# Evening out VectorE's work over the slots of an attention body, and moving ScalarE's loads, in a two-layer decoder kernel

## The chip, the cores and the metric

The kernel runs on one core of a Trainium2 chip. The metric is the device time of one execution in microseconds (us). Three executions of the kernel before took 2007.12, 2007.74 and 2007.95 us; the median is 2007.74.

## The reference: what is computed

```python
# B=16 sequences, S=256 tokens, H=512, 16 heads of 32; fp32 throughout
ln = layernorm(x, ln1);   q, k, v = split(ln @ w_qkv + b_qkv)
x  = x + merge(softmax(mask(q @ k.T / sqrt(32))) @ v) @ w_ao + b_ao          # layer 1: self attention
ln = layernorm(x, ln2);   q = ln @ w_q + b_q;   k, v = split(ctx @ w_kv + b_kv)
x  = x + merge(softmax(mask(q @ k.T / sqrt(32))) @ v) @ w_co + b_co          # layer 2: cross attention
x  = x + gelu(layernorm(x, ln3) @ w1 + b1) @ w2 + b2                         # perceptron
# non-local block over x and ctx: theta, phi, g projections, W = theta.T phi / 512, y = W g, scale, + x
```

All matrix products of fp32 values are made from two halves each (`_h` and `_l`, upper and lower part), as three matmuls: high*high, high*low, low*high (`product`, lines 64 to 68).

## The kernel before, in words

The batch of 16 sequences is cut into 8 blocks of two sequences (512 tokens: four row tiles of 128). The program has three stages:

- 16 short steps at the start (`step`) that fold weights of the non-local block.
- **Attention**: 17 bodies, k = 0 to 16. Bodies 0 to 7 do self attention of blocks 0 to 7, bodies 8 to 15 cross attention, body 16 drains. Each body has eight **slots**, h = 0 to 7.
- The perceptron and the rest of the non-local block (`m_slot`).

A slot treats one group of four heads in a pipeline that is several groups deep. TensorE turns the exponentials of the group before (L1071, out `A_tp`), runs two units of the projections (`units_at`: q and k in slots 0 to 3, two v tiles in slots 4 and 6, two output tiles o in slots 5 and 7), then the scores of a coming group (L1055) and last the weighing of the values (L1089). VectorE multiplies the scores by the mask (L1656), takes maxima (L1666), inverts row sums, scales the weighed values (`scaled`, L1694, out `A_cx`), writes one head's exponentials in 32x32 blocks (L1686), and takes the lower halves of q and k out of PSUM (L1639, `A_q_l`, `A_k_l`) or adds the output tile to the residual (L1634, `A_res`). ScalarE makes the exponentials (L1309, eight per slot, n = 0 to 7), copies turned tiles out of PSUM (L1368) and takes the upper halves.

The units of a slot and the weighing use two PSUM banks in turn: the first unit of a slot needs the bank of the second unit of the slot before (so v0 in slot 4 waits until `A_k_l` of k3 is done, and q0 in slot 0 until `A_res` of o3 is done), the second unit needs the bank whose `A_cx` VectorE makes in the same slot.

Beside that each body prepares the next one's normalised rows. VectorE takes row statistics (`row_statistics`, L1604), GpSimd normalises (L774), VectorE turns the rows in 32x32 blocks (L1814, `A_x<-A_x`), ScalarE's queue writes them to HBM in an order that completes the transposition (`write_block`, L1361, `turned<-A_x`, four DMAs of 64 KB per row tile), and SyncE's queue loads them back (`load_pair`, L734, `A_e<-turned` or `A_xt_l<-turned`).

DMAs are issued by SyncE (SPq in the profile, DMA queue q1) and by ScalarE (ACTq, queue q10), in program order on each. In each slot SyncE issues `A_pt<-exponentials` (256 KB, what the weighing of this slot reads), the store of the inverses, the store of the exponentials, and `A_rt<-inverses` (four DMAs; the next slot's `A_cx` needs them). In slots 5 and 6 it also issues `load_pair`, a row tile and the stores of the output. ScalarE's queue has the loads of `load_row` (`A_x<-x`), `load_res` (`A_res<-x`), masks and contexts; each stands in the program behind one of the exponentials, at a place (h, n). Body 7 also takes in the weights of layer 2 in 16 chunks (`chunk_at`, `load_at`): ScalarE makes the upper half, VectorE the lower half of chunks of w_q, GpSimd of the others. Source line numbers are those of the profile of the kernel before.

Of the kernel before, what the change touches and what calls it, by code (L numbers as in the profile page):

```python
# [18 lines left out]
TT = TOK // P  # L19
NB = B // BPB  # L20
# [7 lines left out]
DMA = 16  # L28
# [109 lines left out]
def whole_network(nc, ctx, nl, m1t_dram, inv_dram, p_dram, xt_dram, rows, x1, x2, ctx_t, s_mask, x_mask, s_weights, x_weights, fold_wt, columns,  # L138
# [12 lines left out]
    NU = 2 * NB  # L151
# [5 lines left out]
    EARLY = 6  # L157
    WARM = 14
    KEPT = range(GROUPS - 12, GROUPS)

    with ExitStack() as stack:
        room = Room(nc, stack, "A")
# [144 lines left out]
        def hidden_bank(blk, f):  # L307
# [7 lines left out]
        load_at = {(7, 0): (0, 1), (7, 3): (2, 3), (7, 5): (4, 5), (7, 6): (6, 7), (7, 7): (8,), (8, 0): (9,), (8, 1): (10, 11),  # L315
                   (8, 2): (12,), (8, 3): (13, 14, 15)}

        made, half_ok, ld_c = room.sem("made"), room.sem("half_ok"), room.sem("ld_c")
# [442 lines left out]
        def _(pool):  # L761
# [94 lines left out]
            def slot(r, k, h, a_, b_, own, pv):  # L856
# [405 lines left out]
        def _(act):  # L1262
# [70 lines left out]
            def load_o_copy(t):  # L1333
                act.dma_start(turned_w[KT + t], fold_wt[3][t * P:(t + 1) * P, :]).then_inc(ld_tw[t], DMA)

            def loads(k, r, h, n):

                if by_blocks(k - 1) and (h, n) in ((0, 3), (0, 4), (1, 3)):
                    load_row(k + 1, r + 1, 2 * h + n - 2)
                if NB <= k + 1 < NU and n == 4 and h in (1, 2):  # L1340
                    load_context(r + 1, h - 1)
                if NB <= k < NU and (h, n) == (3, 5):
                    load_mask(r, 1)
                if NB <= k < NU - 1 and (h, n) == (7, 3):
# [12 lines left out]

# [206 lines left out]
        def _(dve):  # L1564
# [176 lines left out]
            def step(n):  # L1741
# [29 lines left out]
                if n in (7, 11, 15):  # L1771
                    biases_of((n - 7) // 4)

            def slot(r, k, h, a_, b_, own, pv):
                even, odd = turns_at(k, h)
                coming, leaves = exists(k, h, 1), exists(k, h, -2)
# [31 lines left out]
                    lower_pair(k, r, halves_at(k, h))  # L1808
                if k == NU and h in (0, 2):
                    lower_pair(k - 1, r - 1, h // 2)  # L1810
                if by_blocks(k) and h in (3, 4) or k == NU - 1 and 3 <= h < 3 + TT:
                    for t in (2 * h - 6, 2 * h - 5) if by_blocks(k) else (h - 3,):
                        dve.wait_ge(ln_x, (r + 1) * TT + (t + 1))
                        dve.transpose(x[:, t, :], x[:, t, :]).then_inc(a_blk, 1)  # L1814
                if k < NU and h in ((0, 1) if k else (1, 2)):
                    row_statistics(r + 1, 0 if h == (0 if k else 1) else 2)
                    row_statistics(r + 1, 1 if h == (0 if k else 1) else 3)
                if k == 0 and h == 2:
                    aggregate(r + 1)
# [13 lines left out]
                    split_raw(3, O_SPLITS[h])  # L1833
                for n in chunk_at.get((k, h), ()):
                    split_chunk(n)
                if k == NU and h == EARLY:
                    early_chunks = m_chunk_at[(k, h)]
                    for f in range(2, EARLY):
                        if f >= 4:
                            split_m_chunk(early_chunks[f - 4])  # L1840
                        activated(0, f, True)
                    for n in early_chunks[2:]:
                        split_m_chunk(n)
                    dve.wait_ge(m1_hi, 1)
                    dve.tensor_tensor(thw_l[:, :], m1[:, :], f32(thw_h[:, :]), ALU.subtract).then_inc(m1_lo, 1)
# [160 lines left out]
```

## Time and profile before

| | us |
|---|---|
| median of 3 executions | 2007.74 |
| the profiled execution | 2011.13 |
| its span, first to last instruction | 2009.3 |
| TensorE busy in it | 1976.2 (98%) |
| VectorE busy | 1470.8 (73%) |
| ScalarE busy | 1162.6 (58%) |
| GpSimd busy | 550.2 (27%) |

The span leaves out 1.83 us of the execution. Durations below are those of this one execution. Matmuls overlap in the pipeline, so a matmul row's length is not what it costs: the distance between starts is. Attention takes from about 107 to 1259 us of the span. In the profile, groups name tiles as out<-in; buffer numbers are left out. PEld is the weight load that goes before a matmul.

### The profile page before, as it was taken

The numbers are of one execution on the slowest core, as the hardware profiler recorded it, in microseconds if no ns is written. First come the engines' busy times: TensorE is split into PE (matmuls) and PEld (weight loads), VectorE is DVE, ScalarE is ACT, GpSimd is POOL, SyncE is SP. The second block draws the span as 40 slices with busy tenths as digits, with TensorE's granted clock in tenths as the row PEclk, the third lists the DMA queues.
The fourth block names the chain that finished last, engine by engine and source line by source line (L and its number), as shares of the span: only waits on it lengthen the run. The fifth ranks groups of instructions, "written<-read, shape, count | busy, mean of one in ns | idle before, by whom it ended". The sixth has DMA issues, their size and how long they took to land. (4 is left out here: it accounts for less than half of the span.)

```text
span 2009.3 us, 41550 instructions
## 1 busy us (share of the span) xinstructions
PE 1976.2 (98%) x13632; PEld 1570.0 (78%) x13632; DVE 1470.8 (73%) x3868; ACT 1162.6 (58%) x3251; POOL 550.2 (27%) x556
## 2 busy tenths in 40 slices
PE   9999999999999999999999998999999999999998
PEld 8877777777776777777777776888888888888887
DVE  7799999999999999899899888564444343435333
ACT  4388878888888888888888788421111121212111
POOL 1012222222224344323423432053132131313000
PEclk9999999999999999999999999999999999999999
DMA  8546667567668867767767734531212212121201
GB/s 279 168 94 139 146 165 155 128 168 161 135 173 193 195 172 173 168 162 180 176 152 183 170 90 116 171 107 35 79 42 68 68 47 78 47 63 52 61 24 48
DMA packets 681720, 252.67 MB, mean 126 GB/s; under 512 B 533312, under 2 KB 626112, under 8 KB 681536
## 3 DMA queue, kind: packets, MB, share of 16 engines
q1 hardware_dynamic: 535616, 195.84, 38.5%
q10 hardware_dynamic: 145920, 54.55, 11.2%
q8 instruction: 95, 1.56, 0.3%
q14 instruction: 89, 0.73, 0.1%
HBM read 167.41 MB, written 82.84 MB: 125 GB/s over the span
## 5 line engine op out<-in xcount | busy, mean ns | idle before, releaser
L1309 ACT ACTIVATE A_p<-A_p,A_nmax 128x256 f32<-128x256 f32 x1024 | 507.1, 500 | 5.4 <-DVE A_res L1634 1.7
L1666 DVE CUSTOM_DVE_ANT_0 A_p<-A_p,A_ma 128x256 f32<-128x256 f32 x1024 | 376.6, 423 | 4.6
L1656 DVE TENSOR_TENSOR A_p<-A_sc,A_mk 128x1024 f32<-128x1024 f32 x256 | 312.3, 1220 | 48.0 <-PE A_tp L1071 47.4
L820 POOL TENSOR_TENSOR A_ct_l<-A_cx,A_ct_h 128x256 fp32r<-128x256 f32 x122 | 114.3, 937 | 652.3 <-DVE A_nmax L1666 639.1
L1368 ACT ACTIVATE A_pt<-A_tp 128x512 f32<-128x512 f32 x396 | 218.5, 588 | 47.2 <-PE A_tp L1071 45.9
L1071 PEld LDWEIGHTS A_tp<-A_ident,A_p 128*128 128x128 f32 x1584 | 178.8, 141 | 71.2 <-ACT A_p L1309 33.0
L1071 PE MATMUL A_tp<-A_ident,A_p 128*128 128x128 f32 x1584 | 222.5, 277 | 1.5 <-DVE A_xt_l L1617 0.7
L1505 ACT ACTIVATE A_mk<-A_tp,A_cols 128x512 f32<-128x512 f32 x62 | 42.8, 690 | 269.1 <-PE A_tp L68 269.0
L1309 ACT ACTIVATION_READ_ACCUMULATOR A_p<-A_p,A_nmax 128x1 f32 x1024 | 197.2, 193 | 0.0
L1505 ACT ACTIVATE A_ma<-A_tp,A_cols 128x512 f32<-128x512 f32 x62 | 42.8, 690 | 242.5 <-PE A_tp L68 242.5
L66 PE MATMUL A_banks<-A_xt_h,A_w_h 128*128 128x512 f32 x384 | 162.2, 422 | 3.4 <-DVE A_res L1634 2.1
L929 POOL TENSOR_TENSOR A_v<-A_v,A_b_row 128x512 f32<-128x512 f32 x32 | 52.7, 1664 | 362.3 <-DMA A_v<-x 362.3
L68 PE MATMUL A_banks<-A_xt_h,A_w_l 128*128 128x512 f32 x384 | 151.1, 394 | 0.0
L67 PE MATMUL A_banks<-A_xt_l,A_w_h 128*128 128x512 f32 x384 | 150.1, 391 | 0.0
L1857 DVE CAST A_h_h<-A_ma 128x512 fp32r<-128x512 f32 x64 | 30.5, 476 | 160.4 <-ACT A_ma L1505 156.7
L1375 ACT ACTIVATE A_cx<-A_cx,A_bias_sum 128x256 f32<-128x256 f32 x128 | 65.2, 510 | 139.8 <-DVE A_cx L1694 139.7
L66 PE MATMUL A_tp<-A_xt_h,A_w_h 128*128 128x512 f32 x368 | 143.4, 390 | 0.2 <-DVE A_xt_l L1871 0.2
L67 PE MATMUL A_tp<-A_xt_l,A_w_h 128*128 128x512 f32 x368 | 143.2, 389 | 0.0
L68 PE MATMUL A_tp<-A_xt_h,A_w_l 128*128 128x512 f32 x368 | 143.2, 389 | 0.0
L1089 PE MATMUL A_banks<-A_pt,A_v 128*32 128x256 f32 x2048 | 137.9, 387 | 4.8 <-DMA A_pt<-exponentials 2.1
L1857 DVE CAST A_h_h<-A_mk 128x512 fp32r<-128x512 f32 x64 | 29.1, 454 | 143.6 <-ACT A_mk L1505 141.5
L66 PE MATMUL A_banks<-A_w_h,A_ct_h 128*128 128x512 f32 x256 | 105.7, 413 | 1.6 <-issue 1.1
(248 smaller groups left out, 5001.7 us busy)
## 6 DMA issues: line engine op xcount, KB each, us to landing
exponentials<-A_ln_shift SPq DMA_DIRECT2D x464, 64.0 KB, 2.7
A_pt<-exponentials SPq DMA_DIRECT2D x116, 256.0 KB, 3.1
A_rt<-inverses SPq DMA_DIRECT2D x512, 32.0 KB, 2.4
x<-A_res SPq DMA_DIRECT2D x64, 256.0 KB, 3.6
A_res<-x ACTq DMA_DIRECT2D x58, 256.0 KB, 4.1
turned<-A_x ACTq DMA_DIRECT2D x224, 64.0 KB, 2.8
A_x<-x SPq DMA_DIRECT2D x54, 256.0 KB, 3.7
A_x<-x ACTq DMA_DIRECT2D x42, 256.0 KB, 3.1
```

What stands on the lines that cost most here:

```text
L66: pe.matmul(out, sh, mh, start=first, stop=False)
L67: pe.matmul(out, sh, ml, start=False, stop=False)
L68: return pe.matmul(out, sl, mh, start=False, stop=last)
L820: pool.tensor_tensor(ct_l[:, f, part], cx[:, :], f32(ct_h[:, f, part]), ALU.subtract).then_inc(c_lo, 1)
L1071: last = pe.transpose(tp[:, n % 2, c * S + t * P:c * S + (t + 1) * P], p[:, g % 2, j, t, c * P:(c + 1) * P], ident[:, :])
L1089: last = pe.matmul(banks[rr, bank, 0:S], v[:, b * TPB + c, f * P + j * HD:f * P + (j + 1) * HD], turned_keys(grp, j, c), start=(c == 0), s ...
L1309: act.activation(p[:, g % 2, j, t, :], p[:, g % 2, j, t, :], ACT.Exp, scale=-1.0, bias=nmax[:, g % 2, j, t:t + 1], accum_out=rsum[:, g % 2 ...
L1368: act.activation(pt[:, moved(grp) + i, :, :], tp[:, n % 2, :].rearrange("p (c s) -> p c s", c=TPB), ACT.Copy)\
L1375: act.activation(cx[:, :], cx[:, :], ACT.Identity, bias=bias_sum[:, layer(k, h, -2), 2, f:f + 1]).then_inc(c_sum, 1)
L1505: act.activation(hf[f % 4], hidden_bank(blk, f), ACT.Gelu_apprx_tanh, bias=b1_col[:, f:f + 1])\
L1656: dve.tensor_tensor(p[:, g % 2, heads, :, :].rearrange("p j t s -> p j (t s)"), sc[:, heads, :], m, ALU.mult)\
L1666: dve.tensor_tensor_reduce(out=a_, in0=a_, in1=ma[:, b, t, :], scale=-1.0, scalar=BIG, op0=ALU.add, op1=ALU.min, accum_out=nmax[:, g % 2, ...
```

## The change

Four things are moved, all in the attention bodies:

1. **VectorE.** In bodies 1 to 14 the four block transposes of the rows stood as two in slot 3 and two in slot 4; now one stands in slot 3, two in slot 4, one at the end of slot 5. The statistics of row tile 0 move from slot 0 to the end of slot 6 of the body before.
2. **ScalarE's stores of turned rows** follow: tile 0 in slot 4, tiles 1 and 2 in slot 5, tile 3 in slot 6 (before: 0 and 1 in slot 4, 2 and 3 in slot 5).
3. **ScalarE's loads** (rows, contexts, masks, residuals, the copies of w_o) go behind the last exponential (n = 7) of a slot, and some to another slot: row tiles 1, 2, 3 from slots 0, 0, 1 to slots 6 and 7 of the body before and slot 0; residual tiles 0 and 1 from slot 2 to slots 0 and 3, tiles 2 and 3 from slot 6 to slot 6 and the start of slot 7.
4. **Body 7.** The first two bias additions of GpSimd go from slot 4 to slot 1 (their loads to slot 0), and the loads of weight chunks 4 and 5 from SyncE's queue (slot 5) to ScalarE's, behind the last exponential of slot 5.

```diff
+    EARLY_ADDS = (NB - 1, NU - 1)
...
-        load_at = {(7, 0): (0, 1), (7, 3): (2, 3), (7, 5): (4, 5), (7, 6): (6, 7), ...
+        load_at = {(7, 0): (0, 1), (7, 3): (2, 3), (7, 6): (6, 7), ...
...
-                if h == (4 if 1 < k < NU - 1 else 1) and k:
+                if h == (1 if k in (1, *EARLY_ADDS) else 4) and k:
                     add_bias(k - 1, r - 1, 0)
                     add_bias(k - 1, r - 1, 1)
...
-                if by_blocks(k) and h in (4, 5):
-                    write_block(k, r, 2 * h - 8 + n // 4, n % 4)
+                tile = {(4, 0): 0, (5, 0): 1, (5, 1): 2, (6, 0): 3}.get((h, n // 4))
+                if by_blocks(k) and tile is not None:
+                    write_block(k, r, tile, n % 4)
...
-                if by_blocks(k - 1) and (h, n) in ((0, 3), (0, 4), (1, 3)):
-                    load_row(k + 1, r + 1, 2 * h + n - 2)
-                if NB <= k + 1 < NU and n == 4 and h in (1, 2):
+                if by_blocks(k) and (h, n) in ((6, 7), (7, 7)):
+                    load_row(k + 2, r + 2, h - 5)
+                if by_blocks(k - 1) and (h, n) == (0, 7):
+                    load_row(k + 1, r + 1, 3)
+                if NB <= k + 1 < NU and n == 7 and h in (1, 2):
                     load_context(r + 1, h - 1)
-                if NB <= k < NU and (h, n) == (3, 5):
+                if NB <= k < NU and (h, n) == (3, 7):
                     load_mask(r, 1)
-                if NB <= k < NU - 1 and (h, n) == (7, 3):
+                if NB <= k < NU - 1 and (h, n) == (7, 7):
                     load_mask(r + 1, 0)
-                if 1 < k < NU and h == (2 if k < NU - 1 else 0) and n in (5, 6):
-                    load_res(k - 1, r - 1, n - 5)
-                if 0 < k < NU and h == 6 and n in (5, 6):
-                    load_res(k - 1, r - 1, n - 3)
+                if 1 < k < NU and (h, n) in (((0, 7), (3, 7)) if k not in EARLY_ADDS else ((0, 5), (0, 6))):
+                    load_res(k - 1, r - 1, int((h, n) in ((3, 7), (0, 6))))
+                if 0 < k < NU and (h, n) in ((6, 7), (7, 0)):
+                    load_res(k - 1, r - 1, h - 4)
+                if k == NB - 1 and (h, n) == (5, 7):
+                    for c in (4, 5):
+                        load_chunk(c)
-                if k == 2 and (h, n) in ((1, 5), (2, 3), (3, 3), (6, 4)):
+                if k == 2 and (h, n) in ((1, 5), (2, 7), (4, 7), (5, 7)):
...
-                if by_blocks(k) and h in (3, 4) or k == NU - 1 and 3 <= h < 3 + TT:
-                    for t in (2 * h - 6, 2 * h - 5) if by_blocks(k) else (h - 3,):
-                        dve.wait_ge(ln_x, (r + 1) * TT + (t + 1))
-                        dve.transpose(x[:, t, :], x[:, t, :]).then_inc(a_blk, 1)
+                if k == NU - 1 and 3 <= h < 3 + TT:
+                    row_blocks(r, h - 3)
+                if by_blocks(k):
+                    for t in {3: (0,), 4: (1, 2)}.get(h, ()):
+                        row_blocks(r, t)
                 if k < NU and h in ((0, 1) if k else (1, 2)):
-                    row_statistics(r + 1, 0 if h == (0 if k else 1) else 2)
+                    if h != 0 or k < 2:
+                        row_statistics(r + 1, 0 if h == (0 if k else 1) else 2)
                     row_statistics(r + 1, 1 if h == (0 if k else 1) else 3)
...
+                if by_blocks(k) and h == 5:
+                    row_blocks(r, 3)
+                if by_blocks(k) and h == 6:
+                    row_statistics(r + 2, 0)
```

`row_blocks(r, t)` is the wait and the transpose that stood in the loop; `load_chunk` on ScalarE waits for the same semaphores and issues the same DMA as SyncE's.

VectorE at the end of slot 3 of a self-attention body, before (`A_k_l` is the lower half of k3, which frees the bank that v0 needs):

```order
1476 L1666 ISA A_p,A_nmax<-A_p,A_ma 128x256
1477 L1666 ISA A_nmax 128x1
1478 L1814 STREAM_TRANSPOSE A_x<-A_x 128x512 x2
1479 L1639 SCALAR_TENSOR_TENSOR A_k_l<-A_banks,A_bias_sum,A_k_h 128x512
1480 L1656 TENSOR_TENSOR A_p<-A_sc,A_mk 128x1024
```

The same place after the change:

```order
1488 L1681 ISA A_p,A_nmax<-A_p,A_ma 128x256
1489 L1681 ISA A_nmax 128x1
1490 L1792 STREAM_TRANSPOSE A_x<-A_x 128x512
1491 L1654 SCALAR_TENSOR_TENSOR A_k_l<-A_banks,A_bias_sum,A_k_h 128x512
1492 L1671 TENSOR_TENSOR A_p<-A_sc,A_mk 128x1024
```

One transpose stands before `A_k_l` instead of two.

ScalarE from the start of slot 6 of a cross-attention body (body 10) to the start of slot 7, before:

```order
1223 L1309 ACTIVATE A_p,A_rsum<-A_p,A_nmax 128x256 x2
1224 L1368 ACTIVATE A_pt<-A_tp 128x512 x2
1225 L1375 ACTIVATE A_cx<-A_cx,A_bias_sum 128x256
1226 L1378 ACTIVATE A_ct_h<-A_cx 128x256
1227 L1309 ACTIVATE A_p,A_rsum<-A_p,A_nmax 128x256
1228 L1368 ACTIVATE A_pt<-A_tp 128x512
1229 L1301 ACTIVATE A_v<-A_banks 128x512
1230 L1309 ACTIVATE A_p,A_rsum<-A_p,A_nmax 128x256 x2
1231 L1283 ACTIVATE A_xt_h<-A_xt_l 128x4x256
```

The same stretch after the change:

```order
1150 L1310 ACTIVATE A_p,A_rsum<-A_p,A_nmax 128x256
1151 L1376 DMA turned<-A_x 32x16x32
1152 L1310 ACTIVATE A_p,A_rsum<-A_p,A_nmax 128x256
1153 L1376 DMA turned<-A_x 32x16x32
1154 L1383 ACTIVATE A_pt<-A_tp 128x512 x2
1155 L1390 ACTIVATE A_cx<-A_cx,A_bias_sum 128x256
1156 L1393 ACTIVATE A_ct_h<-A_cx 128x256
1157 L1310 ACTIVATE A_p,A_rsum<-A_p,A_nmax 128x256
1158 L1376 DMA turned<-A_x 32x16x32
1159 L1383 ACTIVATE A_pt<-A_tp 128x512
1160 L1302 ACTIVATE A_v<-A_banks 128x512
1161 L1310 ACTIVATE A_p,A_rsum<-A_p,A_nmax 128x256
```

Four stores of row tile 3 now stand in slot 6, one behind each of its first four exponentials (the fourth, row 1162, follows the last row shown).

SyncE's queue in slot 5 of body 7, before and after (`A_wst` is the staging tile of the weight chunks, `A_e<-turned` the row pair that is loaded back):

```order
319 L543 DMA A_rt<-inverses 32x4x64 x4
320 L734 DMA A_e<-turned 128x4x256
321 L490 DMA A_wst<-L0_xattn_w_q 128x512
322 L490 DMA A_wst<-L0_xattn_w_kv 128x512
323 L669 DMA A_x<-x1 128x512
324 L503 DMA x1<-A_res 128x512 x2
325 L565 DMA A_pt<-exponentials 128x4x128
```

```order
319 L544 DMA A_rt<-inverses 32x4x64 x4
320 L735 DMA A_e<-turned 128x4x256
321 L670 DMA A_x<-x1 128x512
322 L504 DMA x1<-A_res 128x512 x2
323 L566 DMA A_pt<-exponentials 128x4x128
```

The two chunk loads are gone from SyncE's queue; ScalarE's queue issues them after the eighth store of turned rows in slot 5.

## Rows read from the trace of the kernel before

**Rows 1.** The page: span, and busy time by engine

```profile
span 2009.3 us, 41550 instructions
PE 1976.2 (98%) x13632; PEld 1570.0 (78%) x13632; DVE 1470.8 (73%) x3868; ACT 1162.6 (58%) x3251; POOL 550.2 (27%) x556
```

**Rows 2.** Body 5, slots 3-6: stretch, length, busy PE PEld DVE ACT POOL, clock, DMA, GB/s

```profile
449.63:458.52 8.89, 8.89 (x81) 6.84 (x77) 8.23 (x26) 7.47 (x24) 2.13 (x4) 1.00 0.36 79
458.52:467.88 9.36, 9.15 (x80) 6.87 (x76) 8.85 (x27) 7.76 (x25) 3.13 (x5) 1.00 0.72 127
467.88:476.78 8.90, 8.90 (x80) 6.84 (x76) 7.58 (x24) 7.04 (x23) 2.62 (x3) 1.00 0.79 139
476.78:485.68 8.90, 8.90 (x80) 6.84 (x76) 7.62 (x23) 7.14 (x20) 1.26 (x1) 1.00 0.99 269
```

**Rows 3.** Waits of the weight loads: us in total, times, longest

```profile
PEld A_banks L66 <- DVE A_k_l L1639: 10.1, 16, 1.0
PEld A_banks L66 <- DVE A_res L1634: 4.4, 9, 0.9
PEld A_banks L66 <- DVE A_cx L1694: 2.0, 3, 1.0
```

**Rows 4.** The same by group: v units; idle time before, and who ended it

```profile
L66 PEld LDWEIGHTS A_banks<-A_w_h,A_xt_h 128*128 128x128 f32 x128 | 24.1, 188 | 6.9 <-DVE A_k_l L1639 2.9
L66 PEld LDWEIGHTS A_banks<-A_w_h,A_et_h 128*128 128x128 f32 x128 | 24.1, 188 | 9.7 <-DVE A_k_l L1639 5.5 <-DVE A_res L1634 0.2
```

**Rows 5.** Timeline, body 5, end of slot 3: start, length, idle before

```profile
457.83 1.30 DVE L1814 STREAM_TRANSPOSE A_x<-A_x 128x512 f32<-128x512 f32 x2
459.05 0.71 DVE L1639 SCALAR_TENSOR_TENSOR A_k_l<-A_banks,A_bias_sum,A_k_h 128x512 fp32r<-128x512 f32 x1
```

**Rows 6.** Timeline, body 10: VectorE's A_cx at the start of slot 3

```profile
818.40 0.42 DVE L1694 TENSOR_TENSOR A_cx<-A_banks,A_rt 128x256 f32<-128x256 f32 x1 [0.99 <-DMA A_rt<-inverses]
```

**Rows 7.** DMA of slot 3 of body 5: kind, KB each, us to landing

```profile
A_rt<-inverses SPq DMA_DIRECT2D x4, 32.0 KB, 2.1
```

**Rows 8.** DMA of slot 2 of body 10

```profile
q10 hardware_dynamic: 686, 0.82, 30.9%
A_rt<-inverses SPq DMA_DIRECT2D x4, 32.0 KB, 4.7
```

**Rows 9.** Timeline, body 7, slots 4 to 6, VectorE and GpSimd

```profile
611.29 3.07 DVE L1580 SCALAR_TENSOR_TENSOR A_w_l<-A_wst,A_lns_q,A_w_h 128x512 fp32r<-128x512 f32 x2
622.43 0.89 DVE L1580 SCALAR_TENSOR_TENSOR A_w_l<-A_wst,A_lns_q,A_w_h 128x512 fp32r<-128x512 f32 x1
610.82 3.00 POOL L779 TENSOR_TENSOR A_res<-A_res,A_o_bias 128x512 f32<-128x512 f32 x2
```

**Rows 10.** Busy time by stretch: slots 5 and 6 of body 7

```profile
611.48:621.99 10.51, 9.26 (x81) 6.79 (x77) 10.42 (x26) 8.53 (x27) 5.90 (x5) 1.00 0.63 114
621.99:632.82 10.83, 8.97 (x81) 6.93 (x77) 8.85 (x25) 8.27 (x23) 4.64 (x4) 1.00 0.94 268
```

**Rows 11.** Waits of TensorE for the reloaded exponentials

```profile
PE A_banks L1089 <- DMA A_pt<-exponentials: 2.1, 2, 1.9
```

**Rows 12.** DMA of slot 5 of body 11 (queue: packets, MB, share of 16 engines)

```profile
q10 hardware_dynamic: 4284, 0.53, 38.9%
```

**Rows 13.** DMA of slot 6 of body 11

```profile
q10 hardware_dynamic: 278, 0.51, 16.4%
A_pt<-exponentials SPq DMA_DIRECT2D x1, 256.0 KB, 5.7
```

**Rows 14.** Timeline, body 11, slot 6: SyncE's load, the weighing, ScalarE, VectorE

```profile
916.64 0.43 SPq L565 DMA_DIRECT2D A_pt<-exponentials  x1
923.66 0.64 PE L1089 MATMUL A_banks<-A_pt,A_v 128*32 128x256 f32 x8
916.46 1.09 ACT L1368 ACTIVATE A_pt<-A_tp 128x512 f32<-128x512 f32 x2 [1.40 <-PE A_tp L1071]
914.65 0.69 DVE L1634 TENSOR_TENSOR A_res<-A_banks,A_res 128x512 f32<-128x512 f32 x1
```

More of the change, by code:

```diff
@@ L314, in whole_network @@
         chunk_at.update({(9, n): (12 + n,) for n in range(4)})
-        load_at = {(7, 0): (0, 1), (7, 3): (2, 3), (7, 5): (4, 5), (7, 6): (6, 7), (7, 7): (8,), (8, 0): (9,), (8, 1): (10, 11),
+        load_at = {(7, 0): (0, 1), (7, 3): (2, 3), (7, 6): (6, 7), (7, 7): (8,), (8, 0): (9,), (8, 1): (10, 11),
                    (8, 2): (12,), (8, 3): (13, 14, 15)}
@@ L1334, in load_o_copy, with load_chunk @@
                 act.dma_start(turned_w[KT + t], fold_wt[3][t * P:(t + 1) * P, :]).then_inc(ld_tw[t], DMA)
-            def loads(k, r, h, n):
-                if by_blocks(k - 1) and (h, n) in ((0, 3), (0, 4), (1, 3)):
-                    load_row(k + 1, r + 1, 2 * h + n - 2)
-                if NB <= k + 1 < NU and n == 4 and h in (1, 2):
+            def load_chunk(n):
+                c, t = chunks[n]
+                if chunks[n - KT][0] == 0:
+                    act.wait_ge(w_lo, 4 * KT + chunks[n - KT][1] + 1)
+                else:
+                    act.wait_ge(w_lo2, sum(1 for c_, _ in chunks[:n - KT + 1] if c_))
+                act.dma_start(wst[:, n % KT, :], x_weights[c][t * P:(t + 1) * P, :]).then_inc(ld_s[n % KT], DMA)
+            def loads(k, r, h, n):
+                if by_blocks(k) and (h, n) in ((6, 7), (7, 7)):
[3 more added lines that the diff above has]
+                if NB <= k + 1 < NU and n == 7 and h in (1, 2):
                     load_context(r + 1, h - 1)
-                if NB <= k < NU and (h, n) == (3, 5):
+                if NB <= k < NU and (h, n) == (3, 7):
                     load_mask(r, 1)
-                if NB <= k < NU - 1 and (h, n) == (7, 3):
+                if NB <= k < NU - 1 and (h, n) == (7, 7):
                     load_mask(r + 1, 0)
-                if 1 < k < NU and h == (2 if k < NU - 1 else 0) and n in (5, 6):
-                    load_res(k - 1, r - 1, n - 5)
-                if 0 < k < NU and h == 6 and n in (5, 6):
-                    load_res(k - 1, r - 1, n - 3)
+                if 1 < k < NU and (h, n) in (((0, 7), (3, 7)) if k not in EARLY_ADDS else ((0, 5), (0, 6))):
+                    load_res(k - 1, r - 1, int((h, n) in ((3, 7), (0, 6))))
+                if 0 < k < NU and (h, n) in ((6, 7), (7, 0)):
+                    load_res(k - 1, r - 1, h - 4)
                 if (k, h, n) == (2, 1, 4):
@@ L1352, in loads @@
                     act.dma_start(shift_rows[1], across(ln_biases[1])).then_inc(ld_sh[1], DMA)
-                if k == 2 and (h, n) in ((1, 5), (2, 3), (3, 3), (6, 4)):
-                    load_o_copy(min(h - 1, 3))
+                if k == NB - 1 and (h, n) == (5, 7):
+                    for c in (4, 5):
+                        load_chunk(c)
+                if k == 2 and (h, n) in ((1, 5), (2, 7), (4, 7), (5, 7)):
+                    load_o_copy({1: 0, 2: 1, 4: 2, 5: 3}[h])
             def write_block(k, r, t, n):
@@ L1772, in step, with row_blocks @@
                     biases_of((n - 7) // 4)
+            def row_blocks(r, t):
+                dve.wait_ge(ln_x, (r + 1) * TT + (t + 1))
+                dve.transpose(x[:, t, :], x[:, t, :]).then_inc(a_blk, 1)
             def slot(r, k, h, a_, b_, own, pv):
```

## The prediction

> **What bounds the kernel now.** I read the page first. TensorE is busy 98% of the span [rows 1], so what can be won is the little that it waits. I then cut the attention into slots by the start of the first turned tile, and asked for the busy time of each slot. The reader is to see in body 5 that three of the four slots shown last 8.89 or 8.90 us with TensorE busy throughout, and one 9.36 us [rows 2]. A slot of 8.90 us is TensorE's own pace. Only what is above it can go. Third, the waits of the weight loads, since a matmul row hides its wait in its length: `A_k_l` 10.1 us in 16 waits, `A_res` 4.4 us in 9, `A_cx` 2.0 us in 3 [rows 3]. With the excess of body 7 (10.51 and 10.83 us for slots of 8.90 [rows 10], together 1.61 + 1.93 = 3.5 us, in part the same waits) that is all that the change can reach: some 19 us, 0.9% of the span. VectorE is no bound over a whole body, but it is in some slots: `A_k_l` comes late at the end of slot 3, where two transposes stand before it.
>
> A second resource is nearly used up in one slot: in slot 6 the DMA engines are busy for a share of 0.99, against 0.36 in slot 3 [rows 2].
>
> **The change part by part: what it takes away.**
>
> *Slot 3, one transpose less.* The two take 1.30 us and `A_k_l` starts 1.22 us after the first [rows 5], so one less brings it 0.61 us forward. The wait of v0 for it is 2.9 us over the self and 5.5 us over the cross bodies, 8.4 us [rows 4]. In body 5 the slot is 0.46 us too long (9.36 - 8.90 [rows 2]), less than 0.61: it goes wholly. The longest of these waits is 1.0 us [rows 3]; such a one has a second cause, seen in body 10, where `A_cx` of slot 3 came 0.99 us late, held by `A_rt<-inverses` [rows 6]. That DMA takes 2.1 us to land where ScalarE's queue loads nothing [rows 7], but 4.7 us in slot 2 of body 10, where a context and two residual tiles (1 MB) share the engines [rows 8]. The change takes the two residual tiles, half of it, out of slot 2, so I count that cause as gone. I take 8.0 of the 8.4 us; if the DMA part stays, four or five waits keep 0.4 us each, and it is 6.4.
>
> *Other waits for VectorE.* `A_k_l` has 10.1 - 8.4 = 1.7 us left, `A_cx` 2.0 us. Slot 0 loses one `row_statistics`, and slots 1 and 2 of body 2 and slot 2 of the cross bodies lose loads. I take 1.5 us of the 3.7; bounds 0 and 3.7.
>
> *Body 7.* VectorE's two chunk splits take 3.07 us, a single one later 0.89 us. Beside the pair run GpSimd's two bias additions, 3.00 us [rows 9]. With these in slot 1 the pair should cost 1.8 to 3.07 us; GpSimd's split of the context moves into the same place, so the low end isn't sure. VectorE then also enters slot 4 0.61 us earlier. Slot 5, 1.61 us too long, gets back 1.5 us; bounds 0.6 and 1.6. Slot 6 is 1.93 us too long because the weighing waits 1.9 us for `A_pt<-exponentials` [rows 10, 11]. SyncE issues it behind two chunk loads, which now go by ScalarE's queue. Both queues' bytes pass the same engines at a share of 0.94, so I count nothing; bounds 1.0 us won (they start about 1.5 us sooner) and 0.5 lost.
>
> The gain is 8.0 + 1.5 + 1.5 = 11.0 us, between 7 and 14.
>
> The Trainium skill, "DMA: Bandwidth & Descriptors", section "Issuing engines are not separate DMA queues", says that DMAs from different issuing engines run on the same 16 DMA engines and interleave, so that a second issuer saves only issue time. By it the two chunk loads on ScalarE's queue bring no bandwidth, which is the zero above. This trace agrees as far as `A_rt<-inverses` on SyncE's queue landed 2.6 us later while ScalarE's queue was loading [rows 7, 8].
>
> **What it adds.** *Four stores into slot 6.* Row tile 3's stores of turned rows come from slot 5 to slot 6 in 14 bodies. In slot 5 of body 11 ScalarE's queue moved 4284 packets, 8.4 such stores of 512 packets, in 38.9% of 8.89 us = 3.46 us of all sixteen engines [rows 12]: 0.41 us each, 1.65 us for four. Slot 6 has no such room. The weighing of slot 6 needs `A_pt<-exponentials`, issued at 916.64 and landed 5.7 us later, at 922.3; the weighing starts at 923.66 [rows 13, 14], so body 11 has 1.3 us of slack. Bodies 7 and 14 have none: theirs are the two waits of [rows 11]. Against the stores stand the two residual loads that were in slot 6: 16.4% of 8.90 = 1.46 us [rows 13]; they now come behind its last exponential or in slot 7, and part of that may be relief for `A_pt`.
>
> Per body: three of four stores are issued before `A_pt` lands, 3 x 0.41 = 1.23 us; slack, between 0 and 1.3, taken as 0.4; relief by the loads that left, a quarter of 1.46, about 0.4. That leaves 0.4 to 0.45 us; I take 0.45. Bounds are 0 and 1.65 us. For 14 bodies that is 6.3 us, between 0 and 23.
>
> The same crowding delays the store of the inverses and so `A_rt`, and with it `A_cx` in slot 7 and q0's bank in slot 0 of the next body (`A_res`, 4.4 us of waits already [rows 3]). As TensorE is then late by the same 0.45 us, I charge it once.
>
> *ScalarE held by the fourth transpose.* Tile 3 is turned after `A_res` of slot 5, which ends at 915.3 in body 11; one transpose of 0.65 us more, and ScalarE's first store can go at 916.0. ScalarE waits for it behind its first exponential. But it sits idle 1.40 us before its copies at 916.46 [rows 14], so about 0.5 us of delay is left, and TensorE's third turned tile comes 2.3 us later than that: nothing. Without that cover it would be 0.5 us in 14 bodies, 7 us.
>
> *Other added work.* One transpose in slot 5 and one statistics in slot 6 of VectorE: slots with 7.58 and 7.62 us busy of 8.90 [rows 2], 0.65 us each fits. Nothing waits behind them except the next slot's mask, which waits for TensorE anyway. Loads behind n = 7 instead of n = 3 to 6 are issued up to 1.5 us later, all for work at least a slot away: nothing. Two row tiles move into the busy slots 6 and 7: in the upper bound above.
>
> **Sum.** -11.0 + 6.3 = -4.7 us against the profiled span of 2009.3: 2004.6. The profiled execution took 2011.13, 3.4 us over the median of the runs, and the stalls are the same in kind, so I subtract the same 4.7 from the median 2007.74: 2003.0 us.
>
> **Rivals.**
>
> *A. The stores cost nothing.* They slip in where the two residual loads were, 1.65 against 1.46 us. For it: the sums nearly balance. Against: the stores come before `A_pt` lands and the loads came mostly after. Time 2007.74 - 11 = 1996.7.
>
> *B. DMA takes back what VectorE gives.* The stores cost 0.8 us a body, 11.2 us in all; time 2007.9, no change. For it: share of 0.99 in slot 6 [rows 2], and the 2.6 us that 1 MB cost `A_rt`. Against: the loads that left.
>
> *C. Slower.* One mechanism: TensorE waits at the weighing of slot 6 and again for q0's bank in slot 0, since the reloads of exponentials and inverses queue behind 1.65 us of stores and an earlier row tile. From (11 + 4) / 14 = 1.1 us a body on, the kernel is slower than measurement noise. At 1.3 us a body it costs 18.2 us; time 2007.74 + 7.2 = 2014.9. For it: two bodies have no slack at all [rows 11], and 1 MB of loads delayed `A_rt` by 2.6 us, nearly their whole length. Against: body 11 has 1.3 us.
>
> The Trainium skill, "DMA: Bandwidth & Descriptors", section "Queues, rings and completion order", says that each DMA engine goes round-robin over the queue rows it has work for, packet by packet. By it each of ScalarE's small stores would pass between SyncE's packets at once and SyncE's reload would pay in full, 1.65 us less slack, which is rival C. Rows 8 agree in kind, no row here shows it for stores of this size in a full slot.
>
> *D. The move has no effect on TensorE,* because `A_k_l` is held by ScalarE's `A_k_h` and not by the transposes. Then about 3 us of gain remain against 6.3 of cost: 2011. Against it: in body 5 `A_k_l` follows the transposes without idle time [rows 5]. I count it with C and B.
>
> **How the numbers follow.** Forecast 0.45 (2003.0; own range 1999 to 2007), A 0.14, B with half of D 0.21, C with the rest 0.20. A difference under 0.2%, 4 us, can't be told from none here. Below 2003.7 lie A and somewhat over three quarters of the forecast: 0.14 + 0.36 = 0.50. Within 4 us: 0.09 of the forecast and 0.19 of B: 0.28. Slower: 0.22. The range reaches from 1996, just under A, to 2013, which leaves out the worse half of C, about 0.1, and as much below.
>
> **What would show it.** Right: slot 4 of the bodies lasts 8.9 us, the weight loads' wait for `A_k_l` falls from 10.1 to about 1 us; slot 5 of body 7 lasts about 9 us; `A_pt<-exponentials` of slot 6 lands up to 1 us later than 5.7, and slot 6 lasts some 9.3 us on the mean of the bodies. Wrong: slot 6 at 9.7 us or more, or `A_res` waits well above 4.4 us (C); slot 6 at 8.9 everywhere (A); `A_k_l` waits unchanged (D).

## The result, and the profile after

The changed kernel took 2020.13 us on the median of 6 runs, the kernel before 2007.85 in 6 runs beside it. The ratio is 1.0059, with a 95% interval of 1.0046 to 1.0072: 11.8 us slower. The forecast was 2003.0, with a range up to 2013. The profiled execution took 2017.02 us and is the shortest of the six, while the one before took 2011.13, 3.3 us above its median. So the two traces differ by 5.9 us of span, about half of the loss; where times are added up below, the ratios of the runs count and the traces show the place.

The page of the changed kernel, answering to [rows 1]:

```profile
span 2015.2 us, 41550 instructions
PE 1976.5 (98%) x13632; PEld 1569.6 (78%) x13632; DVE 1471.2 (73%) x3868; ACT 1164.4 (58%) x3251; POOL 548.9 (27%) x556
```

The work is the same to a thousandth; only waits have changed. To see where, I took the distance between the starts of the first turned tiles of neighbouring slots, subtracted 8.90 us (9.30 in body 15), and summed over bodies 1 to 14 and slot 0 of body 15. In us above TensorE's own pace:

| slot | 0 | 1 | 2 | 3 | 4 | 5 | 6 | 7 | sum |
|---|---|---|---|---|---|---|---|---|---|
| before | 5.1 | 1.4 | 1.4 | 0.7 | 8.9 | 2.9 | 2.7 | 0.3 | 23.3 |
| changed | 13.3 | 0.1 | 1.3 | -0.1 | 0.2 | 1.8 | 5.7 | 6.0 | 28.3 |

Slot 4 won 8.7 us, slots 1, 3 and 5 together 3.2; slots 0, 6 and 7 lost 16.9. Body 5 shows it. Busy time by stretch in the changed kernel, slots 3 to 7 of body 5 and slot 0 of body 6 (columns as in [rows 2]):

```profile
453.75:462.64 8.89, 8.89 (x81) 6.85 (x77) 8.14 (x26) 7.39 (x24) 2.05 (x4) 1.00 0.49 105
462.64:471.52 8.88, 8.88 (x80) 6.84 (x76) 8.35 (x26) 7.99 (x26) 3.02 (x5) 1.00 0.56 107
471.52:480.41 8.89, 8.89 (x80) 6.84 (x76) 8.00 (x25) 6.23 (x21) 2.73 (x3) 1.00 0.78 139
480.41:489.44 9.03, 8.96 (x80) 6.92 (x77) 8.20 (x25) 7.88 (x23) 1.39 (x1) 1.00 1.09 278
489.44:498.68 9.24, 9.06 (x80) 6.79 (x77) 7.35 (x25) 7.14 (x22) 2.80 (x3) 1.00 0.92 211
498.68:508.47 9.79, 9.17 (x80) 6.88 (x77) 9.70 (x27) 8.35 (x28) 2.33 (x2) 1.00 0.71 185
```

The same last two stretches in the kernel before:

```profile
485.68:494.58 8.90, 8.90 (x80) 6.84 (x76) 8.01 (x24) 8.22 (x26) 3.79 (x4) 1.00 0.65 149
494.58:503.48 8.90, 8.90 (x80) 6.84 (x76) 8.72 (x27) 7.38 (x24) 1.43 (x2) 1.00 0.75 197
```

Slot 4 is at 8.88 us where [rows 2] had 9.36. But slot 6 now has a DMA share of 1.09 and slot 7 one of 0.92, and slots 6, 7 and 0 are 0.13, 0.34 and 0.89 us too long. The share adds up the time from start to end of every packet, so above 1 it says that packets on one engine overlap.

Waits of the changed kernel (us in total, times, longest), answering to [rows 3, 11]:

```profile
DVE A_cx L1709 <- DMA A_rt<-inverses: 17.6, 14, 2.2
PEld A_banks L66 <- DVE A_res L1649: 13.6, 15, 1.1
PEld A_banks L66 <- DVE A_cx L1709: 5.6, 13, 1.2
PEld A_banks L66 <- DVE A_k_l L1654: 0.2, 1, 0.2
PE A_banks L1090 <- DMA A_pt<-exponentials: 3.2, 6, 0.9
ACT A_p L1310 <- DVE A_x L1792: 25.4, 15, 2.1
```

The first of them in the kernel before:

```profile
DVE A_cx L1694 <- DMA A_rt<-inverses: 11.0, 18, 1.7
```

The weight loads' wait for `A_k_l` fell from 10.1 us to 0.2. `A_res` went from 4.4 us in 9 waits to 13.6 in 15, `A_cx` from 2.0 to 5.6. Of the 14 waits of `A_cx` for `A_rt` in the changed kernel, 13 stand in slot 7, 16.1 us; before, slot 7 had 7 of them, 3.2 us, and slot 3 had 8, which are gone. The way there can be followed in body 11. VectorE's first `A_cx` of slot 7 and the weight load of q0 in slot 0 of body 12, in the kernel before:

```profile
927.64 0.42 DVE L1694 TENSOR_TENSOR A_cx<-A_banks,A_rt 128x256 f32<-128x256 f32 x1 [0.55 <-DMA A_rt<-inverses]
935.15 0.19 PEld L66 LDWEIGHTS A_banks<-A_xt_h,A_w_h 128*128 128x128 f32 x1 [0.73 <-DVE A_res L1634]
```

and in the changed kernel:

```profile
933.11 0.42 DVE L1709 TENSOR_TENSOR A_cx<-A_banks,A_rt 128x256 f32<-128x256 f32 x1 [1.22 <-DMA A_rt<-inverses]
940.61 0.19 PEld L66 LDWEIGHTS A_banks<-A_xt_h,A_w_h 128*128 128x128 f32 x1 [1.04 <-DVE A_res L1649]
```

`A_rt` holds VectorE some 3 us into slot 7, 0.67 us longer than before. From there to the last `A_res` VectorE has no idle time in the changed kernel, and that `A_res` frees q0's bank. Slot 7 is 0.34 us longer than before and q0's wait 0.31: together the 0.65 us by which VectorE is later. The wait that TensorE shows in slot 0 is a DMA's lateness of slot 6, passed on by VectorE. `A_rt` is loaded back after the store of the inverses has landed, and this store is issued 2.5 to 2.7 us into slot 6 on the mean of the bodies in every kernel here. So I took from each trace when it lands, and when the last of the four `A_rt` lands, in us after the start of slot 6, as means over 12 bodies (2 to 6 and 8 to 14). The full table stands behind the experiments; before it is 7.68 and 11.46, changed 8.40 and 12.88.

### The profile page after: what moved, and what is told of

It reads as the page before. It is cut to its first block and busy times, and to the rows that moved or that the text cites. A ratio compares the mean times of both kernels' runs of the same rounds, so it can differ in the third digit from the quotient of the medians.

```text
span 2015.2 us, 41550 instructions
## 1 busy us (share of the span) xinstructions
PE 1976.5 (98%) x13632; PEld 1569.6 (78%) x13632; DVE 1471.2 (73%) x3868; ACT 1164.4 (58%) x3251; POOL 548.9 (27%) x556
```

## The experiments

Each ratio is against the kernel before on the same chip, from 5 rounds, with its 95% interval. Its median moved from 2007.9 to 2011.1 us between the groups, so the ratios are what to compare; 0.001 is 2.0 us.

**1. Loads back.** ScalarE's loads at their old places (those that the change moved in body 7 stay), nothing else:

```diff
-                if by_blocks(k) and (h, n) in ((6, 7), (7, 7)):
-                    load_row(k + 2, r + 2, h - 5)
-                if by_blocks(k - 1) and (h, n) == (0, 7):
-                    load_row(k + 1, r + 1, 3)
+                if by_blocks(k - 1) and (h, n) in ((0, 3), (0, 4), (1, 3)):
+                    load_row(k + 1, r + 1, 2 * h + n - 2)
...
```

> The changed kernel with ScalarE's loads at their places of before; VectorE's order, the four stores of row tile 3 in slot 6 and body 7 as changed. In the changed kernel slots 6, 7 and 0 are together 16.9 us longer than before over bodies 1 to 15 (+3.0, +5.7, +8.2 us), slot 4 is 8.7 us shorter. Theory S (the four stores in slot 6 make A_pt and A_rt late): all three excesses stay, time 2018 to 2022 us. Theory L (the loads that were moved into slots 6 and 7 do it): they go, time about 2003 us. If both share it in proportion to bytes in slots 6 and 7 (1 MB of stores in... 256 KB of stores in small packets against 512 KB of row tiles): 2008 to 2014 us.

Measured: 1.0024 (1.0014 to 1.0035). 0.0035 of the loss of 0.0059 goes, 7.0 us. Neither theory holds alone.

**2. Transposes and stores back.** Two transposes in slot 3, two in slot 4, no store in slot 6.

> The changed kernel with the four transposes and the stores of the turned rows as before (two in slot 3, two in slot 4); ScalarE's loads, the statistics and body 7 as changed. Theory S: the excess of slots 6, 7 and 0 (16.9 us) goes and the wait of v0 in slot 4 (8.7 us) comes back: 2012 us or less, down to 2006. Theory L: the excess stays and v0's wait comes on top: 2028 us.

Measured: 1.0009 (1.0000 to 1.0018). Again neither theory holds alone: slot 0 is still 9.8 us too long in this trace, against 13.3, so the loads have a part in it without the stores. Slot 4 is 3.8 us too long and not 8.9 as before, although all transposes stand as before. In the cross bodies its excess fell from 5.7 to 1.3 us, and no `A_cx` of slot 3 waits for `A_rt` any more: that part went with the loads, as the prediction had it.

**3 and 4. The other order of VectorE.** Row tile 1 is turned behind `A_k_l`; its stores keep their old places. In 3 the loads are as changed, in 4 as before:

```diff
-                    for t in {3: (0,), 4: (1, 2)}.get(h, ()):
+                    for t in {3: (0,), 4: (2, 3)}.get(h, ()):
                         row_blocks(r, t)
...
-                if by_blocks(k) and h == 5:
-                    row_blocks(r, 3)
+                if by_blocks(k) and h == 3:
+                    row_blocks(r, 1)
```

> The changed kernel, but VectorE turns row tile 0 in slot 3 before A_k_l, row tile 1 in slot 3 behind A_k_l, tiles 2 and 3 in slot 4; all sixteen stores stand in slots 4 and 5 as before. ScalarE's loads as changed. Slot 3 has 0.6 us of idle VectorE in the changed kernel, so the transpose behind A_k_l should fit and slot 4 stay at 8.9 us. Theory S: slots 6, 7, 0 lose the 16.9 us of excess: about 2003 us. Theory L: they keep it: about 2020 us.

> As the kernel with row tile 1 turned behind A_k_l and the stores as before, but also with ScalarE's loads at their places of before. Both theories: no stall in slots 6, 7, 0 beyond those of before (5.1 us in slot 0, 2.7 in slot 6), v0's wait of 8.7 us gone, body 7 about 1 us better: 1998 to 2000 us. If it is above 2004, VectorE's transposes were not what v0 waited for, or one behind A_k_l costs as much as one ahead of it.

Measured: 3 is 0.9996 (0.9986 to 1.0006), 4 is 0.9970 (0.9959 to 0.9982). With the changed placement of tile 3 in place of this one the pair was 1.0059 and 1.0024. So the loads cost 0.0035 in one pair and 0.0026 in the other, and the changed placement, most of it tile 3's (tiles 1 and 2 move too), costs 0.0063 and 0.0054: two causes that add up. The aim of the change, an early `A_k_l`, is reached without any DMA in a new place.

**5. Only the stores' place.** On kernel 4, with tile 3 turned in slot 4 but stored in slot 6:

```diff
-                if by_blocks(k) and h in (4, 5):
-                    write_block(k, r, 2 * h - 8 + n // 4, n % 4)
+                tile = {(4, 0): 0, (4, 1): 1, (5, 0): 2, (6, 0): 3}.get((h, n // 4))
+                if by_blocks(k) and tile is not None:
+                    write_block(k, r, tile, n % 4)
```

> The kernel with row tile 1 turned behind A_k_l and ScalarE's loads as before (2004.3 us, ratio 0.9970), changed in one thing: the four stores of row tile 3 stand behind exponentials 0 to 3 of slot 6 instead of 4 to 7 of slot 5. Row tile 3 is still turned in slot 4, so ScalarE doesn't wait for VectorE there. Theory D (the place of the four DMAs crowds slot 6): most of the 10.4 us between this kernel's base and the changed kernel with the loads back (2014.8 - 2004.3): 2012 to 2015 us, ratio 1.002, slots 6, 7 and 0 together some 10 us longer. Theory A (ScalarE's waits for the fourth transpose, 25.4 us in 15 waits in the changed kernel, make its exponentials and so the inverses late): 2004 to 2006 us, ratio 0.997 to 0.998.

Measured: 0.9967 (0.9955 to 0.9979). Four stores "in slot 6" cost nothing, so my theory D fell as it was put. Three differences to kernel 1 were left. The one that no run takes by itself: kernel 5 has only four stores in slot 5 (tile 2), kernel 1 has eight there (tiles 1 and 2). The other two come from when tile 3 is turned. ScalarE runs ahead of TensorE: its exponentials 0 and 1 of slot 6 are done before TensorE's slot 6 begins. When tile 3 is turned early, the first two stores leave there, in body 11 3.6 and 3.1 us before the slot. When it is turned at the end of slot 5, they leave 0.2 and 0.6 us into the slot, and ScalarE is held up. ScalarE in body 5 of the changed kernel, slot 6 starting at 480.41:

```profile
480.65 0.31 ACTq L1376 DMA_DIRECT2D turned<-A_x  x1
481.00 0.51 ACT L1310 ACTIVATE A_p<-A_p,A_nmax 128x256 f32<-128x256 f32 x1 [1.77 <-DVE A_x L1792]
481.05 0.59 ACTq L1376 DMA_DIRECT2D turned<-A_x  x1
481.68 1.09 ACT L1383 ACTIVATE A_pt<-A_tp 128x512 f32<-128x512 f32 x2
```

**6 and 7. Held exponential or late stores.** On kernel 1, ScalarE makes exponential 1 first and then waits and issues both stores, in time in which it is idle anyway:

```diff
-                if by_blocks(k) and tile is not None:
+                if by_blocks(k) and tile is not None and (h, n) != (6, 0):
+                    if (h, n) == (6, 1):
+                        write_block(k, r, tile, 0)
                     write_block(k, r, tile, n % 4)
```

> The changed kernel with ScalarE's loads back at their old places (2014.8 us, ratio 1.0024; row tile 3 turned at the end of slot 5), changed in one thing: ScalarE makes exponentials 0 and 1 of slot 6 first and then waits for the fourth transpose and issues the first two stores, both in the 1.4 us in which it waits for TensorE anyway. So its exponential 1 is no longer held up, and the two stores still go out just ahead of the reload A_pt and the store of the inverses. Theory A (the held exponential): back to the level of the kernels with tile 3 turned in slot 4, 2005 us, ratio 0.997. Theory B (two stores issued 3.4 us later than where the tile is turned in slot 4, directly ahead of A_pt and the inverses in a slot with a DMA share of 1.0): stays at 2013 to 2015 us, ratio 1.002.

On kernel 5, both stores go out early and only the hold is added, `act.wait_ge(y_ok, (r - 1) * TT + 2)` behind them in front of exponential 1:

> The kernel with row tile 3 turned in slot 4 and its four stores in slot 6 (2005.0 us, ratio 0.9967), changed in one thing: ScalarE issues the first two of these stores behind exponential 0 and then waits there until VectorE has done A_res of slot 5 (0.6 us before the end of the fourth transpose in the changed kernel), so exponential 1 of slot 6 is held up by 1 us or more while the stores go out early. Theory A: 2011 to 2014 us, ratio 1.000 to 1.002. Theory B: 2005 to 2006 us, ratio 0.997.

Measured: 6 is 1.0013 (1.0004 to 1.0022), 7 is 0.9970 (0.9961 to 0.9980). In 6 the waits for `A_x` are gone and most of the loss stays; in 7 ScalarE is held by half as much as in the changed kernel and nothing is lost. So theory B holds and A falls, as far as half a hold can tell. ScalarE's waits in kernel 7:

```profile
ACT A_p L1310 <- DVE A_res L1651: 12.6, 15, 1.7
```

The DMAs of slot 6 of body 11 where the stores leave early (kernel 5; queue, packets, MB, share; then count, KB, us to landing):

```profile
q10 hardware_dynamic: 1323, 0.62, 24.8%
A_pt<-exponentials SPq DMA_DIRECT2D x1, 256.0 KB, 6.1
inverses<-A_turned_inv SPq DMA_DIRECT2D x1, 16.0 KB, 5.1
```

and where they leave late (kernel 6):

```profile
q10 hardware_dynamic: 2356, 0.72, 33.5%
A_pt<-exponentials SPq DMA_DIRECT2D x1, 256.0 KB, 6.0
inverses<-A_turned_inv SPq DMA_DIRECT2D x1, 16.0 KB, 6.0
```

1033 packets more, two stores' worth, and the 16 KB of inverses take 0.9 us longer. On the mean of the 12 bodies it is the same: 8.46 against 7.52 us into the slot. Two stores at the 0.41 us worked out from [rows 12] are 0.82 us. But kernel 5 also has the emptier slot 5. Kernel 4, with eight stores in slot 5 like kernel 6 and none of these in slot 6, lies between, at 7.92 us, and in its slot 6 of body 11 the store takes even less:

```profile
inverses<-A_turned_inv SPq DMA_DIRECT2D x1, 16.0 KB, 4.7
```

One body scatters by half a microsecond (in the changed kernel, with late stores, it is 5.2 in body 11), so the means count: the late stores cost the inverses' store between 0.5 us (against kernel 4) and 0.9 us (against kernel 5). `A_pt` takes as long in both here; on the mean it lands at 7.7 in kernel 6, at 7.1 in kernel 5, but also at 7.7 in kernel 4, which has no such stores in the slot. That doesn't tell.

**8 to 10. Which load.** On kernel 4 (0.9970), with only the row tiles 1 to 3 moved as in the change (kernel 8), only the residual tiles (9), and only row tile 1, to behind exponential 7 of slot 6 (10, the edit shown):

> The same base (2004.3 us), changed in one thing: ScalarE's loads of row tiles 1, 2 and 3 stand in slots 6, 7 and 0 behind the last exponential as in the changed kernel; residual tiles, contexts and masks as before. All of ScalarE's loads together cost 4.6 us on this base (2008.9 - 2004.3), 5.1 us of it in slot 0. Theory R (the row tile in slot 6 delays the inverses' way, and so A_cx of slot 7 and A_res): the whole 4.6 us, 2008 to 2010 us. Theory Q (the residual tiles, the last of which now loads in slot 7): 2004 to 2005 us.

> The same base, changed in one thing: the four residual tiles load in slots 0, 3, 6 and 7 as in the changed kernel; row tiles, contexts and masks as before. Theory R: 2004 us or, since slot 6 loses part of a load, 1 to 2 us less. Theory Q: 2008 to 2010 us.

> The kernel with row tile 1 turned behind A_k_l and the loads as before (2004.3 us, ratio 0.9970), changed in one thing: row tile 1 (256 KB) loads behind the last exponential of slot 6 instead of in slot 0 of the next body. Moving all three row tiles cost 0.27% (5.5 us). Theory R1 (the row tile in slot 6, where the DMA share is 1.0, makes A_rt and so A_cx of slot 7 late): the whole, 2009 to 2010 us, ratio 0.9995, slot 0 some 6 us longer. Theory R2 (row tile 2 in slot 7, beside the reload of the second row pair): nothing, ratio 0.997.

```diff
+                if by_blocks(k) and (h, n) == (6, 7):
+                    load_row(k + 2, r + 2, 1)
-                if by_blocks(k - 1) and (h, n) in ((0, 3), (0, 4), (1, 3)):
+                if by_blocks(k - 1) and (h, n) in ((0, 4), (1, 3)):
                     load_row(k + 1, r + 1, 2 * h + n - 2)
```

Measured: rows 0.9997 (0.9987 to 1.0007), residual tiles 0.9982 (0.9973 to 0.9991), row tile 1 alone 0.9996 (0.9987 to 1.0005). Row tile 1 alone costs 0.0026, 5.2 us, as much as all rows with 0.0027. Slot 0 is 6.3 us longer than in kernel 4, where theory R1 said some 6; R2 fell. The residual tiles' 0.0012 has an interval that overlaps that of kernel 4, so it stays open whether they cost anything. Waits with row tile 1 alone moved:

```profile
DVE A_cx L1708 <- DMA A_rt<-inverses: 15.2, 23, 1.7
PEld A_banks L66 <- DVE A_res L1648: 9.8, 14, 1.1
```

**11. The new order alone.** The kernel before, with row tile 1 turned behind `A_k_l` and nothing else (three lines).

> The kernel before, changed in one thing: row tile 1 is turned in slot 3 behind A_k_l instead of ahead of it. It has none of the statistics, loads, stores or body 7 of the change. Slot 4 should lose 7 to 8 of its 8.9 us of excess. Theory T (only VectorE's order gives the gain): 2003 to 2004 us, as the base of the other three, ratio 0.997. If the statistics and body 7 carry part of it (in the trace of that base slot 1 is 1.4 and slot 0 1.7 us better, body 7 with 8's first two slots 0.7 us better): 2005 to 2007 us.

Measured: 0.9967 (0.9956 to 0.9977). Theory T holds: it is level with kernel 4, so the statistics and body 7 together give nothing that this can tell from zero. In its trace the wait for `A_k_l` is down from 10.1 us:

```profile
PEld A_banks L66 <- DVE A_k_l L1639: 2.4, 5, 1.0
```

**12. Against the crowding.** Kernel 11, with SyncE's load of row tile 0 behind `load_pair` of slot 6 instead of slot 5:

```diff
-                if by_blocks(k) and h == 5:
+                if by_blocks(k) and h == 6:
                     sp.wait_ge(st_a[0], (turned_before(k, r) + 1) * TPB * (P // 32) * DMA)
```

> The kernel before with row tile 1 turned behind A_k_l (ratio 0.9967, 2004 to 2005 us), changed in one thing: SyncE's load of row tile 0 stands behind the reload of the second row pair (start of slot 7) instead of behind the first (end of slot 5). It takes 256 KB out of slot 6. If the DMA share of 1.0 in slot 6 is what makes A_pt and A_rt late, slots 6 and 0 (4.0 and 5.5 us over in that kernel) lose half or more of their excess: 2000 to 2001 us, ratio 0.995. If the order ahead of A_pt counts and not the share, about the same. If it is the first-come order in slot 7 (the row tile stands ahead of A_pt there, which has 1.8 us of margin), nothing or a loss: 2004 to 2008 us.

Measured: 0.9956 (0.9942 to 0.9969), 8.8 us faster than before and the best here. It is what the expectation said for crowding in slot 6: slot 6's excess fell from 4.0 to 0.9 us and slot 0's from 5.5 to 1.4. Against kernel 11 the intervals overlap, and kernel 11's trace is the slowest of its eight executions. What speaks for a gain of its own is that the last `A_rt` lands earlier here than in any other of the 14 traces. The inverses' store among the DMAs of slot 6 of body 11, in the kernel before and in this one:

```profile
inverses<-A_turned_inv SPq DMA_DIRECT2D x1, 16.0 KB, 5.4
inverses<-A_turned_inv SPq DMA_DIRECT2D x1, 16.0 KB, 4.2
```

`A_cx` of slot 7 in the timeline, and the weight loads' wait for `A_res` over the run:

```profile
920.05 0.42 DVE L1694 TENSOR_TENSOR A_cx<-A_banks,A_rt 128x256 f32<-128x256 f32 x1
```

```profile
PEld A_banks L66 <- DVE A_res L1634: 0.7, 2, 0.5
```

The store takes 4.2 us where it took 5.4 before, `A_cx` waits for nothing, and q0 waits 0.7 us in the whole run instead of 4.4.

The table that sums them up, in the order of its third column (landing in us after the start of slot 6; excess of slots 6, 7 and 0 in us, summed as above, each from the one profiled execution, which is up to 4.6 us off its kernel's median):

| kernel | inverses landed | last `A_rt` landed | slot 6 | slot 7 | slot 0 | ratio |
|---|---|---|---|---|---|---|
| 12, row tile 0 later | 7.07 | 10.86 | 0.9 | 1.1 | 1.4 | 0.9956 |
| before | 7.68 | 11.46 | 2.7 | 0.3 | 5.1 | 1 |
| 7, hold only | 7.55 | 11.57 | 2.1 | 0.8 | 4.6 | 0.9970 |
| 4, loads back, new order | 7.92 | 11.60 | 6.2 | 0.6 | 3.3 | 0.9970 |
| 5, stores early in slot 6 | 7.52 | 11.62 | 1.2 | 0.8 | 6.3 | 0.9967 |
| 11, new order alone | 7.85 | 11.79 | 4.0 | 1.0 | 5.5 | 0.9967 |
| 9, residual tiles moved | 7.59 | 11.80 | 3.2 | 1.9 | 6.6 | 0.9982 |
| 10, row tile 1 moved | 7.77 | 12.01 | 3.0 | 2.7 | 9.6 | 0.9996 |
| 3, new order, loads moved | 7.80 | 12.04 | 4.9 | 1.1 | 8.4 | 0.9996 |
| 2, transposes and stores back | 7.76 | 12.14 | 3.0 | 1.9 | 9.8 | 1.0009 |
| 8, rows moved | 7.79 | 12.29 | 3.6 | 2.7 | 11.0 | 0.9997 |
| 6, late stores, no hold | 8.46 | 12.37 | 5.0 | 2.5 | 10.8 | 1.0013 |
| 1, loads back | 8.51 | 12.49 | 5.7 | 3.9 | 11.0 | 1.0024 |
| changed | 8.40 | 12.88 | 5.7 | 6.0 | 13.3 | 1.0059 |

Slot 0 follows the landing of `A_rt` closely (correlation 0.96 over the 14 traces). Late stores move the inverses' store (7.5 to 7.9 becomes 8.4 to 8.5). Row tile 1, issued 5 to 7 us into the slot, moves mostly the reload behind it: from the inverses to the last `A_rt` it takes 3.7 us in kernel 4, 4.2 in kernel 10, and 4.5 with both in the changed kernel. That second difference is small beside the scatter, as kernel 5 has 4.1 without row tile 1. Slot 6's own excess scatters: kernel 4 has 6.2 us, 4.5 of them in bodies 6 and 7.

## Why the prediction was wrong, step by step

**Slot 3, one transpose less: right.** I took 8.0 us; slot 4 lost 8.7. `A_k_l` now follows a single transpose, in body 5 of the changed kernel:

```profile
461.95 0.71 DVE L1792 STREAM_TRANSPOSE A_x<-A_x 128x512 f32<-128x512 f32 x1
462.58 0.71 DVE L1654 SCALAR_TENSOR_TENSOR A_k_l<-A_banks,A_bias_sum,A_k_h 128x512 fp32r<-128x512 f32 x1
```

Rival D fell with it. The second cause of the waits, `A_rt` in the cross bodies, went too, as counted, and kernel 2 shows that the loads' move did it. But the whole gain did not reach the runs: 11.0 us were taken, the slots 1 to 5 of the traces show 12.0, and kernels 4 and 11 are only 0.0030 and 0.0033 faster than before, 6.0 and 6.6 us. Why more was not won stays open.

**Other waits: a little more than taken,** 2.1 us in slots 1 and 3 for 1.5.

**Body 7: right in sign, not in size.** Slots 5 and 6, answering to [rows 10]:

```profile
617.40:627.02 9.62, 9.26 (x80) 6.80 (x77) 9.31 (x27) 7.52 (x24) 3.62 (x3) 1.00 0.64 114
627.02:637.54 10.52, 9.08 (x81) 6.77 (x77) 9.47 (x26) 8.26 (x24) 3.79 (x4) 1.00 1.10 290
```

Slot 5 got back 0.9 us for the 1.5 expected. In slot 6 the wait for `A_pt` is gone but another stands in its place: TensorE waits for ScalarE's copy of the turned tile. ScalarE had just been held by the fourth transpose for 1.33 us, and the issue of the second store behind it took 1.42 us:

```profile
631.64 0.63 PE L1072 MATMUL A_tp<-A_ident,A_p 128*128 128x128 f32 x4 [1.44 <-ACT A_pt L1383]
```

That the hold is the cause is argued, not tested. Kernel 4 has the change's body 7 and kernel 11 has not, and they are level: the body's gain is too small to be measured in the whole.

**Four stores into slot 6: this step failed.** I took 0.45 us a body, 6.3 us in all, bounds 0 and 23. Measured by kernel 1 against kernel 4, the changed placement costs 0.0054, 10.9 us, 0.8 a body (0.0057 against kernel 5); that is inside the bounds and nearly double of what was taken. Three things in it were wrong.
First, the consumer. I weighed the stores against the slack of `A_pt` at the weighing of slot 6. The store of the inverses, 16 KB issued 1.6 us after `A_pt`, had no slack in half of the bodies, as `A_cx` of slot 7 already waited for `A_rt` before (0.55 us in body 11; 7 waits and 3.2 us in slot 7).
Second, "I charge it once". I argued that TensorE is late in slot 6 by the same amount, so that the lateness of `A_rt` would be covered. TensorE was hardly late there: slot 6 took 3.0 us more in all bodies together, 0.2 us a body, slots 7 and 0 13.9 us more. The term that I set to zero was the large one.
Third, the relief of 0.4 us a body. The row tile that was put into slot 6 is as large as the residual tile that left it, and with only the residual tiles moved (kernel 9) the kernel was no faster: 0.9982 against 0.9970.

**Loads behind n = 7 "nothing": this step failed too.** I looked only at who needs the loaded data ("work at least a slot away") and not at whom the transfer meets on its way. Row tile 1 costs 5.2 us; all loads 5.2 to 7.0.

**ScalarE held: right,** as far as tested, with body 7 open. Kernel 7 shows no cost for half of the hold, and kernel 6 no clear gain from taking all of it away (1.0013 against 1.0024, intervals overlap).

**The rivals.** C had the mechanism: reloads of exponentials and inverses behind stores and an earlier row tile, a wait in slot 6 and again in slot 0. Its price, 18.2 us, was near the 16.9 of the trace and the 17.9 of the ratios (0.0054 and 0.0035); its time, 2014.9, was too short because it too subtracted a gain of 11. Of the signs that the prediction named, slot 6 came out at the 9.3 us of its forecast on the mean of the bodies (8.90 + 5.7/14), and C's sign fired, `A_res` at 13.6 us for 4.4. C was given 0.20 because body 11 had slack at the weighing, which is the wrong place to look for slack. By the Trainium skill, "DMA: Bandwidth & Descriptors", section "Queues, rings and completion order", each DMA engine takes the queues in turn, packet by packet, so ScalarE's small stores would pass at once between SyncE's. The runs agree in kind for the inverses' store, 0.5 to 0.9 us later for two stores of 0.41 us; whether it pays in full they don't tell, and for `A_pt` they tell nothing, as said above.

The sum, put right, goes by the ratios, from before to kernel 4, kernel 1 and the changed kernel: a gain of 0.0030 where 11.0 us were taken, the placement at +0.0054 where 6.3 were taken, the loads at +0.0035 where nothing was. That is -6.0 + 10.9 + 7.0 = 11.9 us; these steps add up to the measured ratio by their making, so they divide the loss and don't prove it. In the profiled executions -12.0 us in slots 1 to 5 and +16.9 in slots 6, 7 and 0 make about +5.0, and body 1 began 1.3 us later; it begins between 131.7 and 135.6 us in the 14 traces, with no relation to the edits. The other 6 us of the loss are in no trace, and why slot 0's excess differs between kernels that are level (3.3 to 6.3 us in kernels 4, 5, 7 and 11) stays open.

## What to carry to other kernels

When a transfer is moved into a slot whose DMA engines are full, look for the smallest and latest DMA there that has no slack, not for the largest, and follow it to the next slots: lateness is paid where the result is used, and an in-order engine between, if it has no idle time, passes it on. A place in the program is not a time: the same four stores behind the same exponentials cost nothing when their data was ready, and 11 us when two of them waited for it and went out some 4 us later (with eight stores instead of four in the slot ahead, a part that is not separated). Before moving work to another slot to free an instruction, try its other side: one transpose put behind `A_k_l` instead of ahead of it gave all that kernel 4 gained, with no DMA touched.

## What the runs showed of the hardware

A DMA share of a slot does not tell the cost: slot 6 of body 5 had 1.09 in the changed kernel and 1.09 in kernel 5, which lost nothing by its stores; on the mean of bodies 2 to 14 it was 1.09 and 1.07. And a 16 KB store that is under way beside two 64 KB stores of the other queue landed 0.5 to 0.9 us later (8.46 us into the slot in kernel 6, 7.92 in kernel 4, 7.52 in kernel 5), where the two take 0.82 us of all sixteen engines.
